# Attention output product in four parts by head pairs, norms by token halves, and all engine lists written anew

## The reference

```
x = x + _L0_xattn_ref(ctx_512, _layernorm(x), ...)   # top-k masked similarity matrix of the context
x = x + _L0_ffn_ref(_layernorm(x), ...)              # gated FFN, 8-bit block quantisation of inputs and weights
x = x + _L1_xattn_ref(_layernorm(x), ctx_512, ...)   # 16 heads, then the output product below
x = x + _L1_ffn_ref(_layernorm(x), ...)              # 32 experts, each token takes one
```

```
ctx_c = jnp.einsum('bhsl,bld->bhsd', attn, kv_r)
ctx_lat = jnp.einsum('bhsd,hkd->bhsk', ctx_c, w_kc_kv)
return ctx @ Wo.T                                    # ctx: ctx_lat with its 16 heads side by side
...
m = jnp.mean(x, axis=axis, keepdims=True)
v = jnp.var(x, axis=axis, keepdims=True)
return (x - m) / jnp.sqrt(v + eps)
```

## Time and profile before

| | us |
|---|---|
| median of 3 runs (580.99 to 582.38) | 582.01 |
| the profiled execution | 582.17 |
| its span on the engines | 580.4 |
| TensorE busy | 496.1 (85%) |
| VectorE busy | 361.8 (62%) |
| GpSimd busy | 248.5 (43%) |
| ScalarE busy | 232.2 (40%) |
| TensorE clock granted, mean | 0.923 |

### The profile page before, as it was taken

One profiled execution on the slowest core, in us unless ns is written; L12 is line 12 of the kernel. 1 busy time (PEld: TensorE's weight loads), 2 busy tenths in 40 slices (PEclk: granted clock), 3 DMA queues, 4 the chain that ended last, 5 costly groups with the idle time before them and its releaser, 6 DMA issues.

```text
span 580.4 us, 9482 instructions
## 1 busy us (share of the span) xinstructions
PE 496.1 (85%) x3221; PEld 324.7 (56%) x3221; DVE 361.8 (62%) x737; ACT 232.2 (40%) x626; POOL 248.5 (43%) x268
## 2 busy tenths in 40 slices
PE   2745597788999979999999899999979999988696
PEld 1634353555655647766557576655666765556342
DVE  2998969449978817786585388757823452330354
ACT  1632232313544342365445314654442246461243
POOL 1784351486777541523132644312244232215166
PEclk9975589969999978999999799999998999997799
DMA  7980010045314120002231000123100012272000
GB/s 268 357 328 1 0 73 0 5 144 162 104 30 152 46 69 0 1 27 62 79 101 37 18 20 1 52 59 95 60 16 31 0 43 61 78 210 67 0 3 18
DMA packets 38256, 41.83 MB, mean 72 GB/s; under 512 B 7168, under 2 KB 33408, under 8 KB 37312
## 3 DMA queue, kind: packets, MB, share of 16 engines
q1 hardware_dynamic: 33840, 36.50, 19.9%
q10 hardware_dynamic: 4080, 3.93, 2.1%
q0 software_dynamic: 288, 0.79, 0.5%
HBM read 34.13 MB, written 7.08 MB: 71 GB/s over the span
## 4 chain that ended last, share of the span: by engine, by line
PE 64%; DVE 17%; POOL 7%; ACT 4%; issue 4%; DMA 2%; SPq 1%; POOLq 0%; DVEq 0%; ACTq 0%
PE qc L712 14%; PE s L712 12%; PE qb L712 10%; PE ga L712 10%; PE ua L712 7%; PE tp L715 6%; PE tp L712 4%; POOL moe L1660 4%; DVE amax L1217 2%; DMA masks<-in_moe_masks 1%; PE ua L715 1%; DVE simwk L1295 1%; DVE top L1293 1%; ACT reg L1122 1%; PE ga L715 1%
## 5 line engine op out<-in xcount | busy, mean ns | idle before, releaser
L1600 POOL TENSOR_TENSOR reg<-reg,rsum 128x512 f32<-128x512 f32 x64 | 66.6, 1056 | 132.0 <-DVE rsum L1370 132.0
L1040 ACT COPY reg<-tp 128x512 f32<-128x512 f32 (+1 forms) x100 | 51.0, 510 | 88.0 <-PE tp L715 58.8
L712 PE MATMUL qb<-reg,wA_hi 128*128 128x256 f16 x384 | 74.2, 288 | 2.0 <-DVE reg L1357 1.4
L1122 ACT ACTIVATE reg<-s,nmax 128x256 f32<-128x256 f32 x128 | 59.4, 475 | 35.3 <-DVE nmax L1363 35.2
L712 PE MATMUL qc<-reg,wM 128*64 128x256 f32 (+1 forms) x384 | 67.1, 395 | 2.1 <-DVE reg L1357 2.0
L715 PE MATMUL tp<-idn,reg 128*128 128x128 f32 x296 | 50.1, 294 | 18.6 <-ACT reg L1078 11.5
L1363 DVE TENSOR_REDUCE nmax<-s 128x2 f32<-128x512 f32 x64 | 41.9, 681 | 35.6 <-PE s L712 35.4
L715 PEld LDWEIGHTS tp<-idn,reg 128*128 128x128 f32 x296 | 35.7, 149 | 35.5 <-ACT reg L1078 14.2
L712 PE MATMUL tp<-reg 128*64 128x256 f32 (+2 forms) x288 | 40.9, 397 | 17.1 <-ACT wM L1061 12.3
L1357 DVE TENSOR_TENSOR reg<-qb,cosq 128x768 f32<-128x768 f32 x32 | 30.5, 953 | 32.1 <-PE qb L712 24.4
L712 PEld LDWEIGHTS qc<-reg,wM 128*64 128x64 f32 (+1 forms) x384 | 37.7, 156 | 21.4 <-issue 11.6
(11 more groups left out here) (210 smaller groups left out, 963.2 us busy)
## 6 DMA issues: line engine op xcount, KB each, us to landing
masks<-in_moe_masks SPq DMA_DIRECT2D x16, 512.0 KB, 3.7
wtile<-wE_d SPq DMA_DIRECT2D x120, 64.0 KB, 1.8
y_d<-masks ACTq DMA_DIRECT2D x15, 256.0 KB, 2.3
wM<-in_att_wq SPq DMA_DIRECT2D x1, 2048.0 KB, 8.0
wtile<-in_wo_t SPq DMA_DIRECT2D x1, 2048.0 KB, 12.1
wE_d<-moe SPq DMA_DIRECT2D x16, 128.0 KB, 1.8
reg<-in_kc_q SPq DMA_DIRECT2D x1, 1536.0 KB, 11.3
reg<-in_qr_t SPq DMA_DIRECT2D x1, 1536.0 KB, 19.2
```

The lines of the kernel that those rows point to most:

```text
L712: return nc.tensor.matmul(dst, lhsT, rhs, start=start, stop=stop, skip_group_check=not check)
L1040: nc.scalar.copy(dst, src).then_inc(bank.drained, 1)
L1122: nc.scalar.activation(attn[p % 2][:, (2 * hh + t) * S:(2 * hh + t + 1) * S], s.tensor[:, t * S:(t + 1) * S], ACT.Exp, bias=nmax[:, o:o + ...
L1600: nc.gpsimd.tensor_tensor(a, a, rsum[:, o:o + 2].unsqueeze(2).to_broadcast([P, 2, S]), ALU.mult).then_inc(attn_ready.sem, 1)
```

## The change

Four edits are made.

- `att_out` on TensorE becomes four steps that add into the same bank, over the head pairs 0 to 3, 4 and 5, 6, and 7. Each waits only for its own context steps, and the lists place each by itself. The matmuls are the same 16.
- Norms 2 and 3 go by halves: statistics, power, product and scaling of half 0 no longer wait for half 1, and the turns in `turn_x` wait half by half. In all norms the two tensor_scalar instructions move from GpSimd to VectorE.
- The loads are a table of their own (`SYNC`), the four small loads that shared a semaphore have three, and the tiles of a group are loaded in two halves.
- All lists of all engines are written in another order. Three places in them that the tables show: the load of all expert weights for the last batch (`load_dense`, 2 MB, into `wGU`) stood behind all tile loads of batch 2 and now stands ahead of them; in the last batch's list on GpSimd `unsort` (gathers from `y_d`) stood behind `attention(3,7,1)` and now stands ahead of `attention(3,7,0)`; at a batch's start GpSimd's norm 3 of the batch before stood behind `attention(b,0,0)` and now stands ahead of it, by halves.

Core of the diff:

```diff
+OUT_PARTS = [(0, 4), (4, 6), (6, 7), (7, 8)]
...
-        ("attention", 0, 7, 0), ("attention", 0, 7, 1), ("unsort", -1), ("result", -1),
+        ("unsort", -1), ("attention", 0, 7, 0), ("attention", 0, 7, 1), ("result", -1),
...
-    ("attn_turn", 3, 6, 1), ("context", 3, 6), ("attn_turn", 3, 7, 0), ("attn_turn", 3, 7, 1), ("context", 3, 7),
-    ("att_out", 3), ("moe_turn", 3), ("logits", 3), ("expert", 3, 0), ("expert", 3, 1), ("expert", 3, 2),
...
+    ("att_out", 3, 0), ("attn_turn", 3, 6, 0), ("scores", 3, 7), ("attn_turn", 3, 6, 1), ("att_out", 3, 1),
+    ("context", 3, 6), ("attn_turn", 3, 7, 0), ("attn_turn", 3, 7, 1), ("att_out", 3, 2), ("context", 3, 7),
+    ("att_out", 3, 3), ("moe_turn", 3), ("logits", 3), ("expert", 3, 0), ("expert", 3, 1), ("expert", 3, 2),
...
+    ("load", "kcq"), ("load", "rnk"), ("load", "moc"), ("load", "awk"), ("load", "gam"), ("load_cxt", 0),
+    ("load", "awq"), ("load", "wq"), ("load_x", 0), ("load", "gate"), ("load", "trs"), ("load", "up"), ("load_x", 1),
+    ("load_cxt", 1), ("load_kr",), ("load", "idn"), ("load", "wo"), ("load", "rtr"), ("load", "sink"),
...
+    ("load_tiles", 1, 4, 1), ("load_cxn", 3), ("load_tiles", 1, 3, 1), ("store_out", 1), ("load_dense",),
+    ("load_tiles", 2, 0, 0), ("load_tiles", 2, 2, 0), ("load_tiles", 2, 1, 0), ("load_tiles", 2, 2, 1),
...
+    if name == "att_out":
+        return ["QC"] if args[1] == 0 else []
...
-        ln_mv = [count(f"ln{i}_mv", 2) for i in range(4)]
-        ln_step = [count(f"ln{i}_step", 4 if i == 0 else 3) for i in range(4)]
-        ln_ready = [count(f"ln{i}_ready", 2 if i == 0 else 1) for i in range(4)]
+        ln_mv = [count(f"ln{i}_mv", T + 2 if i < 2 else 3 * T) for i in range(4)]
+        ln_step = [count(f"ln{i}_step", (2, 1, T, T)[i]) for i in range(4)]
+        ln_ready = [count(f"ln{i}_ready", (2, 1, T, T)[i]) for i in range(4)]
...
+            def load_x(b):
+                if b >= 1:
+                    sp.wait_ge(y2_ready.sem, y2_ready.at(b, 0))
                 sp.dma_start(v3(xb[:, :], T), x[b].rearrange("(t p) d -> p t d", p=P)).then_inc(ld_x.sem, 16)
...
+            def load_mask(n):
+                if n < 2:
+                    sp.wait_ge(w_ready.sem, 2)
+                else:
+                    sp.wait_ge(mask_used.sem, n - 1)
+                sp.dma_start(masks[:, (n % 2) * 1024:(n % 2 + 1) * 1024], moe_masks[n]).then_inc(ld_mask[n % 2].sem, 16)
...
-            def load_tiles(b, g):
+            def load_tiles(b, g, half):
...
-                for i in range(8):
+                for i in range(4 * half, 4 * half + 4):
...
             def adj_qk(b):
                 if b == 0:
-                    pe.wait_ge(ld_adj.sem, 64)
+                    pe.wait_ge(ld_aw.sem, 32)
...
             def turn_x(key, ready):
                 b = key[1]
-                pe.wait_ge(ready.sem, ready.at(b, T))
                 pe.wait_ge(TP.drained, TP.free(key))
-                for c in range(C):
-                    for t in range(T):
+                for t in range(T):
+                    pe.wait_ge(ready.sem, ready.at(b, t + 1))
+                    for c in range(C):
                         last = turn(TP.tensor[:, c * S + t * P:c * S + (t + 1) * P], xnat[:, t * D + c * P:t * D + (c + 1) * P])
                 last.then_inc(TP.filled, 1)
...
-            def att_out(b):
-                pe.wait_ge(TP.drained, TP.done(("context", b, PAIRS - 1)))
-                pe.wait_ge(QC.drained, QC.free(("att_out", b)))
+            def att_out(b, part):
+                lo, hi = OUT_PARTS[part]
+                pe.wait_ge(TP.drained, TP.done(("context", b, hi - 1)))
+                if part == 0:
+                    pe.wait_ge(QC.drained, QC.free(("att_out", b, 0)))
                 for t in range(T):
-                    for p in range(PAIRS):
+                    for p in range(lo, hi):
                         last = mm(QC.tensor[:, t * D:(t + 1) * D], cT[:, p * S + t * P:p * S + (t + 1) * P],
-                                  wF[:, p * D:(p + 1) * D], p == 0, p == PAIRS - 1)
-                last.then_inc(QC.filled, 1)
+                                  wF[:, p * D:(p + 1) * D], t == 0 and p == 0, p == PAIRS - 1, check=False)
+                if hi == PAIRS:
+                    last.then_inc(QC.filled, 1)
 
...
-            def norm(b, i, dst, src, ready):
+            def norm_half(b, i, dst, src, ready, t):
 
                 _, _, r, nb, a1, b1 = ln_small(i)
                 scale, bias = (a1, b1) if i == 0 else (r, nb)
+                nc.scalar.activation(dst[:, t * D:(t + 1) * D], src[:, t * D:(t + 1) * D], ACT.Identity,
+                                     bias=bias[:, t:t + 1], scale=scale[:, t:t + 1]).then_inc(ready.sem, 1)
+
+            def norm(b, i, dst, src, ready):
                 act.wait_ge(ln_ready[i].sem, ln_ready[i].at(b, ln_ready[i].per_batch))
                 for t in range(T):
-                    nc.scalar.activation(dst[:, t * D:(t + 1) * D], src[:, t * D:(t + 1) * D], ACT.Identity,
-                                         bias=bias[:, t:t + 1], scale=scale[:, t:t + 1]).then_inc(ready.sem, 1)
+                    norm_half(b, i, dst, src, ready, t)
 
             def adj_qk(b):
...
-            def moe_norm(b):
-                act.wait_ge(QC.drained, QC.done(("att_out", b)))
-                norm(b, 3, xnat, x3, xn4_ready)
+            def moe_norm(b, t):
+                act.wait_ge(QC.drained, QC.done(("att_out", b, 0)))
+                act.wait_ge(ln_ready[3].sem, ln_ready[3].at(b, t + 1))
+                norm_half(b, 3, xnat, x3, xn4_ready, t)
...
-            def x_norm(b):
+            def x_norm(b, t):
                 if b >= 2:
                     act.wait_ge(xsplit_ready.sem, xsplit_ready.at(b - 2, 2))
-                norm(b, 2, xnat, x2[b % 2], xn3_ready)
+                act.wait_ge(ln_ready[2].sem, ln_ready[2].at(b, t + 1))
+                norm_half(b, 2, xnat, x2[b % 2], xn3_ready, t)
...
             def stats(b, i, src):
-                st, mv = ln_small(i)[:2]
+                st, mv, r, nb = ln_small(i)[:4]
                 for t in range(T):
                     nc.vector.bn_stats(st[:, t, :], src[:, t * D:(t + 1) * D]).then_inc(ln_stats[i].sem, 1)
                 for t in range(T):
                     dve.wait_ge(ln_stats[i].sem, ln_stats[i].at(b, t + 1))
                     nc.vector.bn_aggr(mv[:, t, :], st[:, t, :]).then_inc(ln_mv[i].sem, 1)
+                dve.wait_ge(ln_mv[i].sem, ln_mv[i].at(b, T))
+                nc.vector.tensor_scalar(r, mv[:, :, 1], EPS, None, ALU.add).then_inc(ln_mv[i].sem, 1)
+                nc.vector.tensor_scalar(nb, mv[:, :, 0], -1.0, None, ALU.mult).then_inc(ln_mv[i].sem, 1)
+
+            def stats_half(b, i, src, t):
+                st, mv, r, nb = ln_small(i)[:4]
+                nc.vector.bn_stats(st[:, t, :], src[:, t * D:(t + 1) * D]).then_inc(ln_stats[i].sem, 1)
+                dve.wait_ge(ln_stats[i].sem, ln_stats[i].at(b, t + 1))
+                nc.vector.bn_aggr(mv[:, t, :], st[:, t, :]).then_inc(ln_mv[i].sem, 1)
+                dve.wait_ge(ln_mv[i].sem, ln_mv[i].at(b, 3 * t + 1))
+                nc.vector.tensor_scalar(r[:, t:t + 1], mv[:, t, 1:2], EPS, None, ALU.add).then_inc(ln_mv[i].sem, 1)
+                nc.vector.tensor_scalar(nb[:, t:t + 1], mv[:, t, 0:1], -1.0, None, ALU.mult).then_inc(ln_mv[i].sem, 1)
 
...
-                if t == T - 1:
-                    dve.wait_ge(GA.drained, GA.done(("ffn_down", b, t)))
-                    stats(b, 2, x2[b % 2])
+                dve.wait_ge(GA.drained, GA.done(("ffn_down", b, t)))
+                stats_half(b, 2, x2[b % 2], t)
...
-                stats(b, 3, x3)
+                dve.wait_ge(QC.drained, QC.done(("att_out", b, 0)))
+                for t in range(T):
+                    stats_half(b, 3, x3, t)
...
-                pool.wait_ge(ln_mv[i].sem, ln_mv[i].at(b, T))
-                ts(r, mv[:, :, 1], EPS, None, ALU.add).then_inc(step.sem, 1)
-                ts(nb, mv[:, :, 0], -1.0, None, ALU.mult).then_inc(step.sem, 1)
-                pool.wait_ge(step.sem, step.at(b, 2))
+                pool.wait_ge(ln_mv[i].sem, ln_mv[i].at(b, T + 2))
                 nc.gpsimd.tensor_tensor(r, r, halfneg[:, :], ALU.pow).then_inc(step.sem, 1)
-                pool.wait_ge(step.sem, step.at(b, 3))
+                pool.wait_ge(step.sem, step.at(b, 1))
                 last = nc.gpsimd.tensor_tensor(nb, nb, r, ALU.mult)
...
+            def rstd_half(b, i, t):
+                r, nb = (ap[:, t:t + 1] for ap in ln_small(i)[2:4])
+                pool.wait_ge(ln_mv[i].sem, ln_mv[i].at(b, 3 * t + 3))
+                nc.gpsimd.tensor_tensor(r, r, halfneg[:, 0:1], ALU.pow).then_inc(ln_step[i].sem, 1)
+                pool.wait_ge(ln_step[i].sem, ln_step[i].at(b, t + 1))
+                nc.gpsimd.tensor_tensor(nb, nb, r, ALU.mult).then_inc(ln_ready[i].sem, 1)
```

508 lines of the change are left out of this document (258 added, 250 removed), and 2 rows, old and new, of tables (POOL_TAIL, SYNC).

## The result

The changed kernel takes 569.22 us (median of 4 runs, 566.79 to 575.56) against 582.19 beside it: ratio 0.9761, interval 0.9738 to 0.9783, 2.4% faster. The highest of the four runs, 575.56, had a mean clock of 0.928 against 0.946 to 0.955 in the others and is not in the ratio; without it the median is 568.42. The forecast was 561, 551 to 571. The profiled execution took 568.42 us, 13.8 less than that of before.

A forecast was written before the change was run, and what follows sets the result against it. TensorE, busy 85% of the span, was taken as the bound, with gains only where it waits or runs slowly. Terms summed to -20.4 from the profiled 582.17, giving 561.8, about 561 us against the median; range 551 to 571 for 0.8.

The forecast's parts named there:

- forecast -4.4 to `project(0,0)`: From kernel start to the first project of batch 0: setup -1.6 and start of batch 0 -2.8 us.
- together -1.6: Setup: later small loads +1.4 and fewer VectorE-GpSimd collisions -3.0 us; bounds +4.8 and -4.5.
- The start of batch 0 itself: Norm 2 by halves and earlier x_turn -2.0, project(0,1) ahead of to_keys(0,0) -0.8: -2.8 us (-1 to -4).
- +1.4: Setup: small loads now behind kc_q delay the first matmul by 1.4 us; bounds 0.5 and 4.8.
- fewer collisions: Setup: VectorE and GpSimd lists reordered, mask step near 2 us instead of 5.13; -3.0 us, bounds 0 and -5.
- Start of batch 1: cxt wait gone -2.6, clock back earlier -2.4, halves of norm 2 -0.5: -5.5 us (-2.6 to -8.3).
- new stalls: Inside the batches, not placed: new list orders cost +2.5 us (-1 to +6), one to three microseconds in some batches.
- Starts of batches 2 and 3: Norm 2 by halves removes the 1.31 wait, plus some clock: -3.3 us at batch 2, -3.0 at batch 3.
- Rival B: Batch starts keep their low clock, new lists add other waits, some stalls more: 569 to 575 us; chance 0.14.
- Tail: 14 of 16 output-product matmuls move ahead: VectorE's att_out -6.2 us; norm 3 -0.8; together -7.0 (-2.9 to -9.7).
- rival C: Tail: unsort(2) holds up attention(3,7), att_out gains 2.9 at most instead of 6.2: 565 us, within the forecast's range.
- Rival D: Batch starts: GpSimd's attention(b,0,0) waits behind both halves of the previous batch's norm 3, kernel slower; chance 0.04.

The follow-up runs named there:

- run 9: Kernel before, with the turned context of batch 2 loaded behind the fourth store of expert weights instead of the last: 577.64 us, ratio 0.993.
- run 10: Kernel before, with the output product in four parts, in batch 3 placed as in the changed kernel; unsort, loads and norms as before: 581.95 us, ratio 0.999.
- run 4: Changed kernel, with the four parts of the last batch's output product one behind the other behind the last context step: 571.96 us, ratio 0.983.
- run 1: Changed kernel, with adjacency weights, context of batch 0 and gamma issued first, kc_q, rank and expert constants behind them: 571.59 us, ratio 0.981.
- run 5: Kernel of run 2, with adjacency weights, context, gamma and x of batch 0 issued ahead of the large query weights: 567.22 us, ratio 0.972.
- run 2: Changed kernel, with the third weight matrix's four turns in order 0, 1, 3, 2 and ahead of both hidden_turn(0,0,*): 567.74 us, ratio 0.976.
- run 6: Kernel of run 2, with quant_w(0,2) on VectorE behind the last top rounds and the mask step: 567.02 us, ratio 0.974.
- run 12: Changed kernel with edits of run 2, run 5, run 6, rstd(0,1) ahead of dequant_w(0), and output product parts 0 and 1 moved later: 564.47 us, ratio 0.971.
- run 3: Changed kernel with the edits of run 1 and run 2 together: 569.01 us, ratio 0.979.
- run 7: Kernel of run 2, with load_dense (2 MB) back behind all tile loads of batch 2: 572.00 us, ratio 0.982.
- run 11: Kernel of run 2, with norm 2 whole again on VectorE, GpSimd and ScalarE; tensor_scalars stay on VectorE: 574.70 us, ratio 0.989.
- run 8: Kernel of run 2, with ScalarE's norm 2 of half 0 directly ahead of half 1 at all batch starts: 570.70 us, ratio 0.981.

## Why the prediction was right in sign and 8 us off

**The setup (forecast -4.4 to `project(0,0)`, measured +2.4) makes up the whole error of 6.6 us between the two profiles;** the other misses, +2.4 and -1.5 at batches 0 and 1, -0.2, +1.3 and +0.2 behind them and -2.5 for the stalls, cancel. The term that failed is "together -1.6" for the setup. Up to VectorE's second add of `ffn_down` the lists of before took 112.4, 114.4 and 112.7 us (before, runs 9 and 10), the changed ones 117.5 and 114.8 (changed, run 4). So the setup got longer, by 0.4 to 5.1 us; the size is open. The start of batch 0 itself, from VectorE's second add of `ffn_down` to `project(0,0)`, went from 7.3 to 4.7 us, -2.7 against -2.8. Of the setup's steps:

- "+1.4" for the small loads was too small as such (+3.2), and the ring order of the Trainium skill (DMA: Bandwidth & Descriptors, Queues, rings and completion order) was borne out in direction: a weight of 16 KB landed 5.5 us after its issue behind `kc_q` and 2.0 without. But in runs 1 and 5, without this delay, VectorE's second add of `ffn_down` came only 0.1 and 0.5 us earlier than in the changed kernel and run 2.
- "-3.0" for fewer collisions was wrong in sign: the mask step got 1.6 us longer in this pair. Run 9, with the lists of before, had it at 2.25 us, and `project(0,0)` came no earlier (121.8): its length alone decides nothing. Runs 5, 6 and 12 show how it goes: the mask step, the step on y and the tensor_scalars end with GpSimd's large product or at most 0.6 us behind it, so moving the mask step only decided which of them pays. Other steps of VectorE are not held: inside the product from 41.71 to 46.21 of the changed kernel a max8 took 0.73 us and a match_replace 0.40, and inside that from 69.06 to 72.70 the `amax` above took its 2.29, while the tensor_scalar behind it took 1.07 and ended at 72.74. The Trainium skill, SBUF — State Buffer, section SBUF: two separate sides, says this as an exclusive lock for the whole instruction on the port pair that the two share, and only for some kinds of VectorE instructions, those with two SBUF inputs among them. I had taken off most of the price; the runs agree with the lock.
- The turns of the third weight matrix I had not looked at: about +1.0 by their order and +1.2 by the clock during them (runs 2 and 4).
- `qr_t` is issued at 27.34 instead of 6.30 and lands for `fold_k` at 38.88; the third weight matrix, which takes the place of its data, begins on VectorE at 69.35 and not at 66.94. That this sets the end of the setup with the others removed is read from the rows of run 12 (its wait of 4.44) and wasn't tried.

**Start of batch 1** (-5.5, measured -3.1 in the stretch that ends with it). The mechanism was right: the wait for `cxt` is gone, in the 20 us ahead of `project(1,0)` TensorE is idle 1.8 us instead of 3.8 at a clock of 1.00 instead of 0.85, and alone the edit gives 3.3 us in the stretch (run 9). The rest of batch 0 took it back: TensorE is idle there 8.2 us instead of 5.1. These are the "new stalls" of +2.5, right in size and all in one batch. That -3.1 was measured all the same is mostly luck: the first 20 us of batch 0 ran at 1.00 in this profile and at 0.85 in that of before. In runs 3 and 7, with the same lists there, they ran at 0.84 and 0.85 as before, and the stretch took 97.0 and 96.8, only 0.3 to 0.5 under 97.3.

**Starts of batches 2 and 3** (-3.3 and -3.0, measured -4.8 and -3.2). The numbers are near, the shares are not all the norm's. The -4.8 begins with 20 us in which the clock rose from 0.89 to 1.00, and that belongs to the start of batch 1: run 9 has the same rise without any change to the norm, and took 3.0 less. With norm 2 whole again (run 11) 2.4 of the 4.8 and 1.0 of the 3.2 came back; these are shown for the halves. What the other 2.2 of batch 2 are is not shown; the kernel before took 107.0 there at a clock of 1.00 (run 10), so some 1.1 of them is clock. The profile of run 8 speaks for the early statistics and power and against the overlap on ScalarE. Rival B, a clock that stays low at the starts, fell: on both sides of the starts of batches 1 and 2 it was 1.00 in all profiles with the changed lists but run 11. Its 569 to 575 is near where the median and the highest run lie, but as far as the profiles show for another reason, the clock at the start of batch 0 and in batch 3.

**Tail** (-6.2, measured -4.9; norm 3 -1.3 against -0.8). The steps came as described: part 0 3.7 us, `result(2)` 0.2 us ahead of TensorE, the early dense load as the condition. Its price is 3.9 (run 7), that of the parts 5.7 to 6.9 (run 4), and without the other edits the parts give nothing in the total (run 10): rival C was the right rival for the kernel before. The missing 1.3 is mostly clock: run 2 has the same steps and idle time here (8.54 us against 8.45) and took 95.8 at a clock of 1.00, which is -6.1. At the end of the span, though, only 0.3 us of norm 3's 1.3 came through, with the clock at 0.88 instead of 0.91.

**Rival D** did not occur: in the 20 us around the step in each of the last three batches no matmul waits for GpSimd.

## What to carry to other kernels

Where an engine is nearly always busy, read its clock beside its waits, place by place: here one wait of 2.6 us taken away gave 3.3 in its stretch and 4 in the total, and a norm chain whose idle time adds up to some 3 us cost 7. Steps that another engine holds up are not made cheaper by moving them to another of its long instructions; ask which step pays in their place, and which steps are not held at all. (To put only such steps beside GpSimd's products was not tried.) And cut the traces at the same events before reading the total, and take more than one profile of the same list: one setup came to `project(0,0)` at 118.7 to 121.8, the other at 119.5 and 122.2, and most of these terms were smaller than that.

## What the runs showed of the hardware that was not expected

The same list with the same idle time takes different times: batch 1 of the kernel before took 110.3 us at a clock of 0.96 and, in run 9, with 3.97 us idle in both, 107.3 at 1.00. Runs of the changed kernel lay between 566.8 and 570.0 (mean clock 0.946 to 0.955; 575.6 at 0.928), those of run 2 between 564.3 and 572.4 (0.943 to 0.957), those of before between 579.7 and 584.6 (0.926 to 0.941). At full clock the stretches repeat to 0.1 us (105.0 in ten profiles for batch 2). In batches 0 to 2 the clock was below 1.00 only within 20 us of a batch's start, in all profiles but that of run 1, where batch 1 had 1.0 us more idle time in its middle and 0.95 there. Why the same start has 0.85 in one execution and 1.00 in the next stays open.

VectorE's tensor_scalar of 128x2 took 0.17 us alone and 2.48 beside GpSimd's product, one of 128x64 took 0.20 and 3.71, and the mask step 0.86 and up to 6.68. For these kinds it doesn't matter how small the instruction is, only how much of GpSimd's is left; max8, match_replace and a maximum over 128x2048 kept their times (0.73, 0.40 and 2.29 us) inside such products.
